# A graph convolution's edge loop: four buffers instead of two, sixteen ring rows instead of eight

## What is computed

```python
h = silu(edge_scalars @ fc_w1 * (1.0 / sqrt(8)))        # first layer, 8 -> 64
w = h @ fc_w2                                           # second layer, 64 -> 256: w_a w_b w_c w_d
xg0, xg1 = y0[edge_src], y1[edge_src]                   # gathered node rows, 64 + 3 x 64
mid0 = w_a * xg0 * ea0                                  # ea: 4 numbers of each edge
mid1 = w_b * sum_c(xg1[c] * ea1[c])
mid2 = w_c * xg0 * ea1[c]
mid3 = w_d * ea0 * xg1[c]
agg = segment_sum(concat(mid0, mid1, mid2, mid3), edge_dst)
```

## Time and profile before

| | |
|---|---|
| median of three runs | 5430.12 us (5427.34 to 5434.84) |
| the profiled execution: its time, its span | 5423.88 us, 5421.8 us |
| TensorE, VectorE, ScalarE, GpSimd busy | 71%, 57%, 46%, 55% of the span |
| mean granted TensorE clock | 0.780 of full speed |
| the edge loop of `conv_edges` | about 224 to 2012 us of the span |
| bytes moved | 536.50 MB, mean 99 GB/s |

### The profile page before, as it was taken

One profiled execution on the slowest core, in us unless ns is written; L12 is line 12 of the kernel. 1 busy time (PEld: TensorE's weight loads), 2 busy tenths in 40 slices (PEclk: granted clock), 3 DMA queues, 4 the chain that ended last, 5 costly groups with the idle time before them and its releaser, 6 DMA issues. The chain is left out here.

```text
span 5421.8 us, 84838 instructions
## 1 busy us (share of the span) xinstructions
PE 3823.1 (71%) x21623; PEld 2881.3 (53%) x21623; DVE 3070.9 (57%) x7560; ACT 2487.0 (46%) x7826; POOL 3004.2 (55%) x3072
## 2 busy tenths in 40 slices
PE   2788989888898887556666667766266666666670
PEld 1577777777777766334444444543144444444450
DVE  4766666666666655445455554557355555445558
ACT  1566666666666652233333333344133333333342
POOL 2255555555555530356666666664566666666645
PEclk7899999999999998766676666678666666767675
DMA  3322222222222222334444444432344443444424
GB/s 113 107 71 72 72 71 72 72 71 71 69 72 72 72 62 90 121 97 116 119 120 118 113 118 120 120 104 72 113 114 119 119 116 114 120 120 119 121 71 145
DMA packets 253329, 536.50 MB, mean 99 GB/s; under 512 B 65503, under 2 KB 139674, under 8 KB 252917
## 3 DMA queue, kind: packets, MB, share of 16 engines
q0 software_dynamic: 136768, 380.16, 25.4%
q1 hardware_dynamic: 109128, 145.00, 8.4%
q10 hardware_dynamic: 7020, 6.40, 0.3%
HBM read 489.95 MB, written 41.38 MB: 98 GB/s over the span
## 5 line engine op out<-in xcount | busy, mean ns | idle before, releaser
L1124 POOL DMA_INDIRECT arena<-h_rows,idx x1856 | 1882.6, 1014 | 1191.1 <-issue 487.2
L1288 PE MATMUL ps<-arena,z 128*128 128x264 f32 x3712 | 1551.8, 567 | 380.0 <-DVE arena L1397 227.1
L640 POOL DMA_INDIRECT arena<-y_rows,idx x928 | 879.6, 948 | 850.1 <-DVE arena L825 605.1
L1288 PEld LDWEIGHTS ps<-arena,z 128*128 128x128 f32 x3712 | 932.2, 275 | 660.1 <-DVE arena L1397 300.5
L715 ACT ACTIVATE arena<-arena 128x128 f32<-128x128 f32 x3712 | 1131.8, 389 | 287.4 <-DVE arena L809 201.2
L1405 DVE TENSOR_TENSOR z<-ps,z 128x264 f32 x928 | 400.0, 431 | 1106.1 <-PE ps L1288 621.1
L771 PEld LDWEIGHTS ps<-arena 128*128 128x128 f32 x5568 | 811.3, 201 | 55.6
L771 PE MATMUL ps<-arena 128*128 128x128 f32 x5568 | 812.2, 284 | 0.0
L1192 ACT ACTIVATE z<-z 128x256 f32<-128x256 f32 x928 | 379.8, 409 | 942.4 <-PE ps L1288 545.1
L768 PE MATMUL ps<-arena 128*128 128x256 f32 x1856 | 627.5, 421 | 206.8 <-ACT arena L715 153.8
L1184 ACT ACTIVATE z<-iota,dst_x 128x128 f32<-128x128 f32 x1856 | 641.5, 393 | 24.4
(11 more groups left out here) (229 smaller groups left out, 3049.7 us busy)
## 6 DMA issues: line engine op xcount, KB each, us to landing
z<-lo_rows SPq DMA_DIRECT2D x116, 512.0 KB
arena<-h_rows,idx POOLq DMA_INDIRECT x1856
arena<-y_rows,idx POOLq DMA_INDIRECT x928
z<-seg_rows SPq DMA_DIRECT2D x232, 64.0 KB
h_rows<-arena SPq DMA_DIRECT2D x98, 132.0 KB, 1.7
arena<-h_rows SPq DMA_DIRECT2D x98, 132.0 KB, 2.3
res_rows<-z SPq DMA_DIRECT2D x98, 128.0 KB, 1.7
arena<-res_rows SPq DMA_DIRECT2D x98, 128.0 KB, 2.1
```

The costliest lines, as they stand in the source:

```text
L640: pool.indirect_dma_start(out=s.ring[:, r, 0:width], out_offset=None, in_=table, in_offset=bass.IndirectOffsetOnAxis(ap=s.idx[:, u, n:n + ...
L1124: pool.indirect_dma_start(out=ring[:, u * SCORED + n, :], out_offset=None, in_=h_rows, in_offset=bass.IndirectOffsetOnAxis(ap=s.idx[:, u, ...
L1288: last = t.matmul(ps[:, bank[q % 4], 0:ROW], sel[:, q % SELS, k, :], ring[:, u * SCORED + 2 * q + k, :], start=(k == 0), stop=(k == 1))
```

## The change

What it does, part by part:

1. `msg`, `eq` and `sel` have four buffers, the second layer four PSUM banks of one pair each (both slots in one bank). The sums keep banks 6 and 7, `h2` and the first layer's PSUM their two.
2. The order runs further ahead. TensorE, for pair n: `first` of pairs n+6 and n+7 (each second time), `second(n+3)`, `collect(n)`. VectorE: `messages(n+1)`, `select(n+3)`, `add(n-1)`. ScalarE: `weights(n+2)`, `silu` of pairs n+4 and n+5, and at a group's pair 0 the staging of the next group (before, at pair 3). The waits follow: what waited for the buffer of two pairs back now waits for that of four, and `select` waits for ScalarE's scalings, no more for a collection.
3. The gathered rows have a ring of sixteen, a semaphore for each; GpSimd may gather for pair p when the messages of pair p-8 are made.
4. The second layer's weights are laid out as 128 x 512, `fc_w2` in the upper left and the lower right, zero elsewhere, and each slot's matmul takes all 128 partitions of `h2`: the other slot's numbers meet zeros.
5. `select` is one TENSOR_TENSOR of 256 instead of two TENSOR_SCALAR of 128.
6. The arena is shared out anew; `eq` and `e8` have memory of their own.

```diff
-RING = 8
+RING = GROUP
...
-        s.ring = s.arena[:, 4096:4096 + RING * FEAT].rearrange("p (r f) -> p r f", f=FEAT)
-        s.wk = s.arena[:, 6144:8192]
-        s.e8 = s.arena[:, 8192:8192 + 2 * P].rearrange("p (u e) -> p u e", u=2)
-        s.h2 = s.arena[:, 8448:8448 + 4 * P].rearrange("p (q a e) -> p q a e", q=2, a=2)
-        s.eq = s.arena[:, 8960:8960 + 4 * P].rearrange("p (b k n) -> p b k n", b=2, k=2)
-        s.edge_x = s.arena[:, 9472:9472 + 4 * SLOT_COLS].rearrange("p (c s) -> p c s", c=4)
+        s.wk = s.arena[:, 4096:6144]
+        s.sel = s.arena[:, 0:4096].rearrange("p (b k c n) -> p b k c n", b=4, k=2, c=4)
+        s.msg = s.arena[:, 4096:8192].rearrange("p (b k f) -> p b k f", b=4, k=2)
+        s.ring = s.arena[:, 8192:8192 + RING * FEAT].rearrange("p (r f) -> p r f", f=FEAT)
+        s.h2 = s.arena[:, 12288:12288 + 4 * P].rearrange("p (q a e) -> p q a e", q=2, a=2)
+        s.edge_x = s.arena[:, 12800:12800 + 4 * SLOT_COLS].rearrange("p (c s) -> p c s", c=4)
+        s.eq = sb("eq", [P, 4, 2, P])
+        s.e8 = sb("e8", [P, 2, P])
         s.i8 = sb("i8", [P, 2], I32)
         s.w8 = sb("w8", [P, 8 * P])
-        s.w2 = sb("w2", [P, FEAT])
+        s.w2 = sb("w2", [P, 2 * FEAT])
         s.ps = ctx.enter_context(nc.psum_tensor("ps", [P, 8, 512], F32))
...
-            r = n % RING
-            if n % 2 == 0 and not (isinstance(g, int) and g == 0 and n < RING):
-                pool_wait(pool, s, msg_ok, g * 8 + n // 2 - RING // 2 + 1)
-            pool.indirect_dma_start(out=s.ring[:, r, 0:width], out_offset=None, in_=table,
-                                    in_offset=bass.IndirectOffsetOnAxis(ap=s.idx[:, u, n:n + 1], axis=0)).then_inc(got[r][0], 16)
+            if n % 2 == 0 and not (isinstance(g, int) and g == 0):
+                pool_wait(pool, s, msg_ok, (g - 1) * 8 + n // 2 + 1)
+            pool.indirect_dma_start(out=s.ring[:, n, 0:width], out_offset=None, in_=table,
+                                    in_offset=bass.IndirectOffsetOnAxis(ap=s.idx[:, u, n:n + 1], axis=0)).then_inc(got[n][0], 16)
...
 def landed(eng, got, g, n):
-    arrived, before = got[n % RING]
-    eng.wait_ge(arrived, (g * (GROUP // RING) + n // RING + 1) * 16 + before)
+    arrived, before = got[n]
+    eng.wait_ge(arrived, (g + 1) * 16 + before)
...
-                sp.dma_start(s.w2[h * 64:(h + 1) * 64, 0:FEAT], a["fc_w2"]).then_inc(wt, 16)
+                sp.dma_start(s.w2[h * 64:(h + 1) * 64, h * FEAT:(h + 1) * FEAT], a["fc_w2"]).then_inc(wt, 16)
...
+            def silu(g, u, n):
+                k = g * (IN // 2) + n // 2
+                act.wait_ge(pre_ok, k + 1)
+                if not early(k, 2):
+                    act.wait_ge(w_ok, 2 * (k - 1))
+                nc.scalar.activation(h2[:, n // 2 % 2, :, :].rearrange("p a e -> p (a e)"), ps[:, n // 2 % 2, 0:2 * P], ACT.Silu,
...
-            def weights(g, q, b):
-                pair = g * 8 + 2 * q + b
+            def weights(g, u, n):
+                pair = g * IN + n
                 act.wait_ge(eq_ok, pair + 1)
+                if not early(pair, 4):
+                    act.wait_ge(agg_ok, pair - 3)
...
             def group(g, u, final=False):
-                for q in range(4):
-                    if q < 3:
-                        silu(g, q + 1)
-                    elif not final:
-                        silu(g + 1, 0)
-                    for b in range(2):
-                        weights(g, q, b)
-                    if q == 1 and not final:
+                for n in range(IN):
+                    if not (final and n + 2 >= IN):
+                        weights(*ahead(g, u, n + 2))
+                    if n % 2 == 0 and not (final and n + 4 >= IN):
+                        silu(*ahead(g, u, n + 4))
+                    if n == 0 and not final:
                         stage(g + 1, 1 - u)
             stage(0, 0)
-            silu(0, 0)
+            silu(0, 0, 0)
+            silu(0, 0, 2)
+            for n in range(2):
+                weights(0, 0, n)
...
-            def second(g, q, b):
-                pair = g * 8 + 2 * q + b
-                pe.wait_ge(h_ok, g * 4 + q + 1)
-                if not (isinstance(g, int) and g == 0 and q == 0):
-                    pe.wait_ge(msg_ok, pair - 1)
+            def second(g, u, n):
+                pair = g * IN + n
+                pe.wait_ge(h_ok, g * (IN // 2) + n // 2 + 1)
+                if not early(pair, 4):
+                    pe.wait_ge(msg_ok, pair - 3)
                 for k in range(2):
-                    rows = slice(64 * k, 64 * k + 64)
-                    last = nc.tensor.matmul(ps[:, 2 + 2 * b + k, 0:FEAT], h2[rows, q % 2, b, :], s.w2[rows, 0:FEAT], start=True, stop=True)
+                    last = nc.tensor.matmul(ps[:, 2 + n % 4, k * FEAT:(k + 1) * FEAT], h2[:, n // 2 % 2, n % 2, :], s.w2[:, k * FEAT:(k + 1) * FEAT],
+                                            start=True, stop=True)
                 last.then_inc(w_ok, 1)
...
-            def collect(g, q, b):
-                pair = g * 8 + 2 * q + b
+            def collect(g, u, n):
+                pair = g * IN + n
                 pe.wait_ge(msg_ok, pair + 1)
                 pe.wait_ge(sel_ok, pair + 1)
-                if not (isinstance(g, int) and g == 0 and q == 0):
+                if not early(pair, 2):
                     pe.wait_ge(z_ok, pair - 1)
-                o = ps[:, 6 + b, :]
+                o = ps[:, 6 + n % 2, :]
...
             def group(g, u, final=False):
-                for q in range(4):
-                    if q < 3:
-                        first(g, u, q + 1)
-                    elif not final:
-                        first(g + 1, 1 - u, 0)
-                    for b in range(2):
-                        second(g, q, b)
-                        if isinstance(g, int) and g == 0 and q == 0 and b == 0:
-                            continue
-                        if b:
-                            collect(g, q, 0)
-                        elif q:
-                            collect(g, q - 1, 1)
-                        else:
-                            collect(g - 1, 3, 1)
+                for n in range(IN):
+                    if n % 2 == 0 and not (final and n + 6 >= IN):
+                        first(*ahead(g, u, n + 6))
+                    if not (final and n + 3 >= IN):
+                        second(*ahead(g, u, n + 3))
+                    collect(g, u, n)
             first(0, 0, 0)
+            first(0, 0, 2)
+            second(0, 0, 0)
+            second(0, 0, 1)
+            first(0, 0, 4)
+            second(0, 0, 2)
             run_all(GROUPS - 1, 2, group)
             group(GROUPS - 1, tail, True)
-            collect(GROUPS - 1, 3, 1)
...
-            def select(g, q, b):
-                pair = g * 8 + 2 * q + b
-                if not (isinstance(g, int) and g == 0 and q == 0):
-                    dve.wait_ge(agg_ok, pair - 1)
-                for k in range(2):
-                    last = v.tensor_scalar(eq[:, b, k, :], s.iota[:, :], s.dst_x[:, bass.ds(pair * 2 + k, 1)], None, ALU.is_equal)
-                last.then_inc(eq_ok, 1)
-            def messages(g, q, b):
-                pair = g * 8 + 2 * q + b
-                n = 4 * q + 2 * b
+            def select(g, u, n):
+                pair = g * IN + n
+                if not early(pair, 4):
+                    dve.wait_ge(sel_ok, pair - 3)
+                v.tensor_tensor(eq[:, n % 4, :, :], s.iota[:, :].unsqueeze(1).broadcast_to([P, 2, P]),
+                                s.dst_x[:, bass.ds(pair * 2, 2)].unsqueeze(2).broadcast_to([P, 2, P]), ALU.is_equal).then_inc(eq_ok, 1)
+            def messages(g, u, n):
+                pair = g * IN + n
                 dve.wait_ge(w_ok, pair + 1)
-                landed(dve, got, g, n)
-                landed(dve, got, g, n + 1)
-                w = ps[:, 2 + 2 * b:4 + 2 * b, 0:FEAT].rearrange("p k (q f) -> p k q f", q=4)
-                x = yg[:, n % RING:n % RING + 2, :]
-                m = msg[:, b, :, :]
+                if not early(pair, 4):
+                    dve.wait_ge(agg_ok, pair - 3)
+                landed(dve, got, g, 2 * n)
+                landed(dve, got, g, 2 * n + 1)
...
+            def add(g, u, n):
+                pair = g * IN + n
+                block = dve.value_load(s.blk[0:1, bass.ds(pair * 2, 1)], min_val=0, max_val=BLOCKS - 1)
+                dve.wait_ge(agg_ok, pair + 1)
+                if early(pair, 1):
+                    dve.wait_ge(zero_ok, 1)
+                else:
+                    dve.wait_ge(z_ok, pair)
+                dst = s.z[:, bass.ds(block * 512, 512)]
+                v.tensor_tensor(dst, ps[:, 6 + n % 2, :], dst, ALU.add).then_inc(z_ok, 1)
...
+                for n in range(IN):
+                    if not (final and n + 1 >= IN):
+                        messages(*ahead(g, u, n + 1))
+                    if not (final and n + 3 >= IN):
```

(10 more changed lines are left out.)

60 lines of the change are left out of this document (21 added, 39 removed).

## The result

| | before | after |
|---|---|---|
| median (four runs each) | 5431.33 us (5427.34 to 5434.84) | 5525.4 us (5525.08 to 5528.76) |
| ratio | | 1.0175, 95% interval 1.0162 to 1.0188 |
| profiled execution's span | 5421.8 us | 5523.3 us |
| edge loop, first to last collecting matmul | 226.68 to 2011.31: 1784.6 us | 230.03 to 2112.41: 1882.4 us |
| what follows the loop | 3410.5 us | 3410.9 us |

The account below looks back on a forecast made before the run. TensorE was taken to bound the edge loop, stopped about once a group by late reports. Pairs of 3.29 us save 258 us, less 3 at the start and 20 of remaining stalls: 235 less, 5195 us; range 5165 to 5340, some 0.8.

Parts of the forecast that it names:

- Where the time is lost: Edge loop: 3.846 us a pair against 3.255 undisturbed; late reports stop TensorE about once a group, 274 us to take from.
- Full height, +0.03 a pair: Second layer with 128 rows instead of 64 adds 0.03 us a pair, 14 us in all; bounds 0 and +0.43.
- Rival C: Second layer: full height costs its full 0.43 us, pair 3.685, time 5358 us; chance 0.06.
- Comparison, ScalarE, GpSimd as cover: Edge loop: VectorE's comparison 0.06 us shorter, ScalarE about 2.7 us, GpSimd 21.3 us a group; all fit under TensorE's 3.29-us pair.
- First layer six pairs ahead, nothing on the path: Edge scalars needed before a group's third pair; their gather lands 1.8 us before TensorE asks, so no cost.
- Do late reports still stop TensorE?: Edge loop: up to 3.16 us of lateness costs nothing, the addition falls due next; remaining stalls cost 20 us in all.
- d: Delay of the report that a collection has ended; taken as 3.4 us, 4.8 at the longest.
- A: The main forecast for the edge loop, stalls mostly gone: 5165 (no stall left) to 5230 us; chance 0.62.
- B: Two accumulators keep the stall, TensorE idling before L776 once a group: 157 us above 5175, 5332; chance 0.20.
- Ring of sixteen ... at nothing: The ring of sixteen gathered rows, moved buffers and a larger memset add no time.
- D: Slower: TensorE stands behind the edge-scalar gather at a group's third pair; landing 6 us late gives 5523 us; chance 0.07.

Follow-up runs that it names:

- before_ring16: Kernel before with only sixteen ring rows instead of eight, gathers allowed eight pairs ahead instead of four: 4717.02 us beside 4717.38 of before, ratio 1.000.
- before_full: Kernel before with only the second layer at full height, zero-padded weights, two PSUM buffers kept: 4737.56 us beside 4723.27 of before, ratio 1.0030.
- lead4: Changed kernel, gather for pair p allowed once messages of pair p-4 (not p-8) are made, ring still sixteen: 5127.22 us beside 4717.38 of before, ratio 1.0871.
- no_gather: Changed kernel without the node gathers of groups 1 to 57, reusing the first group's rows: 4752.03 us beside 4717.38 of before.

## Why the prediction was wrong

- **Where the time is lost** was read rightly: 3.255 us an undisturbed pair and 274 us of stock. Without stalls before takes 3.253 a pair (before_ring16), and its loop is 1784.6 - 1509.6 = 275 us shorter. Idle time is not all of it: behind that of 318.8 us the granted clock is 0.50 for 3.4 us and then 1.00 for 27 us; that half of the 3.4 us is lost, 1.7, was my estimate.
- **Full height, +0.03 a pair**: measured +0.038 (before_full). Rival C's 0.43 is not borne out: two half-height passes at a time would have saved 0.43 us a pair, and 0.038 is all that half height saves. The four half-height passes take 0.63 us, which lies between 0.43, two at a time, and the 0.87 of the full-height ones.
- **Comparison, ScalarE, GpSimd as cover**: L810 takes 0.41 us against 0.48, and none of the three stops TensorE on a prompt chip.
- **First layer six pairs ahead, nothing on the path**: right from the second group on, wrong by 9.7 us once. In the first group sixteen node gathers, issued at 1.25 us each, stand ahead of that of the edge scalars; I reckoned the steady state and not the fill.
- **"Do late reports still stop TensorE?" is the step that failed, by its d.** Its slack was nearly right, 3.16 us reckoned and 3.54 measured, and so was what it named as due next, the addition. (Its 0.3 us for the addition's report was an estimate with no row beside it; of the 0.84 to 0.95 us above, 0.15 to 0.26 lie behind the addition's 0.69.) It priced this with the d that it read from before, 3.4 us and 4.8 at most (idle times of VectorE), and came to 20 us in all. In after the report is more than 6 us late in 57 of 58 groups. By the step's own rule 6.7 us (the median of the groups' longest) would cost 6.70 - 3.54 = 3.16 us a group, 58 x 3.16 = 183 us, by an estimate. The loop shows 347 us over the undisturbed 1535.3: 215 of idle time beyond the 9.7 of the start, and some 131 of passes that take longer, for which the step had put nothing in A's sum (half clock stands only in B's, below). I took over as given a delay that had been measured under the old order.
- **"Ring of sixteen ... at nothing"**, and no term at all for TensorE halting inside a collection (160.6 us before L779). Which part of the change makes the reports later, ring, order or something else, stays open. The ring was my suspect, and the rows do not bear it out: 21 of the 49 idle times with four gathers end while GpSimd goes straight on. lead4 and before_ring16, which would have settled it, ran on chip 12. Whether gathers hold up reports at all, and why on some chips only, is open too (no_gather never met a late chip).
- **Rivals.** B, the two accumulators keeping the stall, is there as a mechanism: they hold 77 collections. Only 23.0 us of this show as a wait, since elsewhere TensorE had already halted or came late to it. B had priced it with delays near the slack, as 1 us of idle time and 1.7 us of half speed in each of 58 groups, 157 us above 5175: 5332, on which the range's upper end rests. No run shows losses of that size once a group; in after the loop's mean granted clock is 0.94 and reports are over 6 us late in 57 groups. D gave 5523 for a time, and 5525 was measured, but by another mechanism: its wait took 9.2 us, once. The near agreement is chance.

## What to carry to other kernels

A delay that ends with a "remote" cause is no constant of the surroundings: here it was at most 4.6 us in one kernel and over 6 in the other, and a slack of 3.5 us, enough for most of the old delays, was too short for the new ones. Test tolerance by making the delay by hand, one detour of a report on an idle engine, and measure on the trace how late it came, from the end of the work to the start of what waits for it; the waiting engine's idle time is another number (3.2 us late, 4.27 idle). And price the first group by itself when a step moves ahead, as well as the full height that comes with the extra buffers (16 us here).

## What was unexpected of the hardware

Two sorts of chips: before takes 4715 to 4723 us on 12, 10 and 5 and 5431 to 5433 on 0 and 14, 15% more, with a gather at 0.95 us on either. Of the difference 275 us lie in this loop, where they are idle time and slower passes, and 434 after it (2977.0 in before_ring16 against 3410.5). The granted clock over the span is 0.842 (before_ring16) against 0.780. On the late chip TensorE halts up to 2.5 us at a time (197 times, 0.8 us on average) between passes of one collection that wait for nothing the profile shows. In 73 of VectorE's 117 idle times over 2.5 us it halts too, and these hold 169 of its 191 us without a releaser.
